# A quantized cross-attention product with a LoRA expert layer: the first five row tiles laid out anew

## What is computed

```
def fake_quant(x, scale, zp):
    q = clip(round(x / scale + zp), 0, 255)
    return (q - zp) * scale

xattn(x1, x2) = matmul(fake_quant(x1, ...), fake_quant(x2, ...))
ffn(x)  = x @ W_up.T  +  LoRA delta of the one expert that argmax(x @ gate_w.T + expert_bias) picks
x = x + tanh(g_xattn) * xattn(layernorm(x), ctx_4096)
x = x + tanh(g_ffn)   * ffn(layernorm(x))
```

## Time and profile before

| | |
|---|---|
| median of three runs | 960.24 us |
| the profiled execution: its own time | 959.95 us |
| the profiled execution: span of its instructions | 958.1 us |
| TensorE busy | 936.5 us (98% of the span) |
| VectorE busy | 472.3 us (49%) |
| ScalarE busy | 234.5 us (24%) |
| GpSimd busy | 17.1 us (2%) |

### The profile page before, as it was taken

How to read it: one execution, slowest core, us unless ns; L and a number is a source line. 1 busy time by engine, 2 the same in 40 slices (tenths; PEclk the granted TensorE clock), 3 DMA queues, 4 the chain that set the end, 5 groups by cost and what they waited for, 6 DMA issues and landing times.

```text
span 958.1 us, 12470 instructions
## 1 busy us (share of the span) xinstructions
PE 936.5 (98%) x5253; PEld 501.1 (52%) x5278; DVE 472.3 (49%) x1022; ACT 234.5 (24%) x196; POOL 17.1 (2%) x40
## 2 busy tenths in 40 slices
PE   3999999999999999999999999999999999999998
PEld 2444444444455555555555555555555555555554
DVE  7774757785884715343342615343342615343321
ACT  6975776777650100000000000000000000000000
POOL 0001100000000000000000000000000000000000
PEclk9999999999999999999999999999999999999999
DMA  8999987688652332222223233222223222121211
GB/s 350 422 405 406 377 318 271 227 302 290 221 152 88 111 110 44 88 44 89 44 89 88 66 111 45 88 44 88 45 88 88 61 72 44 45 45 44 44 44 44
DMA packets 77081, 135.26 MB, mean 141 GB/s; under 512 B 61936, under 2 KB 62080, under 8 KB 62720
## 3 DMA queue, kind: packets, MB, share of 16 engines
q1 hardware_dynamic: 71088, 92.74, 30.1%
q0 software_dynamic: 3488, 24.92, 6.7%
q10 hardware_dynamic: 2448, 16.78, 4.3%
HBM read 90.38 MB, written 29.37 MB: 125 GB/s over the span
## 4 chain that ended last, share of the span: by engine, by line
PE 96%; ACT 2%; DVE 1%; DMA 1%; issue 0%; SPq 0%; ACTq 0%
PE bank L1085 71%; PE bank L1003 22%; PE bank L1094 1%; PE bank L980 1%; ACT arena L414 1%; DMA rows<-in_x 1%; DVE bn L598 0%; ACT rows_T L402 0%; ACT halves L384 0%; PE bank L1077 0%; DVE arena L669 0%; SPq L282 0%; PE bank L1100 0%; DVE ln L602 0%; ACT ln L378 0%
## 5 line engine op out<-in xcount | busy, mean ns | idle before, releaser
L1085 PE MATMUL bank<-arena,rows_T 128*128 128x416 f16 (+1 forms) x3840 | 683.4, 339 | 0.0
L1085 PEld LDWEIGHTS bank<-arena,rows_T 128*128 128x128 f16 x3840 | 372.4, 97 | 304.3
L1003 PE MATMUL bank<-arena,rows_T 128*128 128x512 bf16 x999 | 222.8, 381 | 3.7 <-DVE arena L669 2.5
L1003 PEld LDWEIGHTS bank<-arena,rows_T 128*128 128x128 bf16 x1024 | 99.5, 98 | 120.6 <-issue 4.8
L783 DVE SCALAR_TENSOR_TENSOR rows<-bank,derived,rows 128x416 f32<-128x416 f32 (+2 forms) x80 | 49.8, 640 | 213.9 <-PE bank L1085 213.9
L453 ACT ACTIVATE z_stack_T<-bank 96x128 f16<-96x128 f16 x16 | 4.4, 273 | 560.1 <-PE bank L1100 560.1
L598 DVE BATCH_NORM_STATS2 bn<-rows 128x6 f32<-128x512 f32 x124 | 76.7, 678 | 5.9 <-DMA rows<-in_x 5.7
L723 DVE SCALAR_TENSOR_TENSOR route<-bank,derived,scal 128x4 f32<-128x4 f32 x16 | 3.5, 221 | 113.2 <-PE bank L1085 113.2
L659 DVE SCALAR_TENSOR_TENSOR rows<-bank,derived,rows 128x512 f32<-128x512 f32 x60 | 44.7, 748 | 25.0 <-PE bank L1003 24.6
L791 DVE SCALAR_TENSOR_TENSOR rows<-bank,z_back_scale,rows 128x512 f32<-128x512 f32 x64 | 45.1, 746 | 10.6 <-PE bank L1094 6.6
L699 DVE SCALAR_TENSOR_TENSOR halves<-normed,ln,halves 128x2048 f16<-128x2048 f32 x14 | 32.9, 2351 | 29.0 <-ACT halves L447 29.0
(11 more groups left out here) (106 smaller groups left out, 293.0 us busy)
## 6 DMA issues: line engine op xcount, KB each, us to landing
arena<-in_ctx SPq DMA_DIRECT2D x22, 1024.0 KB, 16.4
stage<-in_w SPq DMA_DIRECT2D x17, 1042.0 KB, 5.5
out<-rows ACTq DMA_DIRECT2D x15, 1024.0 KB, 3.9
h_scratch<-rows POOLq DMA_DIRECT2D x11, 1024.0 KB, 9.5
rows<-h_scratch SPq DMA_DIRECT2D x11, 1024.0 KB, 4.9
stage<-in_ctx SPq DMA_DIRECT2D x10, 1024.0 KB, 9.9
rows<-in_x POOLq DMA_DIRECT2D x10, 1024.0 KB, 9.2
normed<-in_w SPq DMA_DIRECT2D x7, 1042.0 KB, 6.5
```

The costliest lines, as they stand in the source:

```text
L1003: mm = mmul(bk, q1T[:, t % 4, kt, :], Q(b, n, kt), start=(kt == 0), stop=(kt == KT - 1 and not slow), skip_group_check=True)
L1085: mm = mmul(bank[c][:, 0:b - a], YT[:, s % 2, yh, kt, :], W(kt, wh, a, b), start=(first and kt == kts[0] and yh == 0 and wh == 0), stop=(k ...
```

## The change

It alters six things, all ahead of row tile 5:

- `BY_V` grows from three halves to six. VectorE copies halves (0,0), (1,0), (2,0), (2,1), (3,0) and (3,1). ScalarE keeps (0,1), (1,1) and both halves from tile 4 on.
- `order` is written out for the first 16 chunks, and TensorE's parts are single steps that mix up to four row tiles; whole chunks begin only at (4, 0).
- The eight zero products that stood between `transposes(0)` and `transposes(1)` stand ahead of `transposes(0)`.
- SP loads row tile 3 ahead of context tile 3, row tile 4 behind context tile 8 (it was behind 13) and row tile 5 behind 13 (it was behind 15).
- ScalarE and VectorE get new orders up to `ctx_round(19)` and `clip(5)`.
- `moments(2)` and `moments(5)` are split in two, so that other work stands between their halves.

```diff
@@ -37,7 +37,7 @@
     BY_PE = 2
     HALF = KT // 2
 
-    BY_V = [(1, 0), (2, 1), (3, 1)]
+    BY_V = [(0, 0), (1, 0), (2, 0), (2, 1), (3, 0), (3, 1)]
     SPARE = 5
     YS = 2.0 ** 9
     WS = 2.0 ** 14
@@ -53,9 +53,8 @@
     h_t = nc.dram_tensor("h_scratch", (TILES - KEEP, P, D), F32).ap()
 
 
-
-    order = [(t, n) for n in range(2) for t in range(LEAD)] + [(LEAD, 0), (LEAD, 1)] + [
-        (t, n) for a in (0, 2) for n in range(2, NCH) for t in (a, a + 1)] + [
+    order = [(1, 0), (0, 0), (2, 0), (2, 1), (0, 1), (3, 0), (1, 1), (2, 2),
+             (3, 1), (1, 2), (0, 2), (0, 3), (1, 3), (3, 2), (2, 3), (3, 3)] + [
         (t, n) for t in range(HEAD, TILES) for n in range(NCH)]
     place = {tn: g for g, tn in enumerate(order)}
     ROT = (0, 1, 2, 3, 4, 7)
@@ -286,18 +285,22 @@
             row(2)
             ctx_tile(1)
             ctx_tile(2)
+            row(3)
             ctx_tile(3)
-            row(3)
             ctx_tile(4)
             ctx_tile(5)
             ctx_tile(6)
             ctx_tile(7)
-            for c in range(8, 14):
-                ctx_tile(c)
+            ctx_tile(8)
             row(4)
+            ctx_tile(9)
+            ctx_tile(10)
+            ctx_tile(11)
+            ctx_tile(12)
+            ctx_tile(13)
+            row(5)
             ctx_tile(14)
             ctx_tile(15)
-            row(5)
             for c in range(16, CT):
                 ctx_tile(c)
             for i in range(KT + 8):
@@ -478,35 +481,38 @@
             quant(0)
             sqrt(1)
             ctx_round(0)
-            half(0, 0)
             quant(1)
             half(0, 1)
+            ctx_round(1)
             sqrt(2)
-            ctx_round(1)
+            ctx_round(2)
             quant(2)
             half(1, 1)
-            ctx_round(2)
-            half(2, 0)
             ctx_round(3)
             ctx_round(4)
             sqrt(3)
             ctx_round(5)
+            ctx_round(6)
             quant(3)
-            ctx_round(6)
             ctx_round(7)
             ctx_round(8)
-            half(3, 0)
-            for c in range(9, 15):
-                ctx_round(c)
+            ctx_round(9)
+            ctx_round(10)
+            ctx_round(11)
+            ctx_round(12)
+            ctx_round(13)
+            ctx_round(14)
             sqrt(4)
+            quant(4)
             ctx_round(15)
-            quant(4)
+            ctx_round(16)
             sqrt(5)
-            ctx_round(16)
+            ctx_round(17)
+            ctx_round(18)
             quant(5)
-            evac(4)
-            for c in range(17, 20):
-                ctx_round(c)
+            half(4, 0)
+            half(4, 1)
+            ctx_round(19)
 
             def period(p, a, b, c):
                 a()
@@ -800,63 +806,68 @@
 
             moments(0)
             quant_scale(0)
-            scalars()
             moments(1)
             clip(0)
             quant_scale(1)
-            moments(2)
+            scalars()
+            half(0, 0)
+            moments(2, 0, 2)
             clip(1)
-            quant_scale(2)
+            moments(2, 2, 4)
             ctx_clip(0)
             ctx_clip(1)
+            quant_scale(2)
+            half(1, 0)
+            ctx_clip(2)
             clip(2)
-            half(1, 0)
             moments(3, 0, 2)
-            ctx_clip(2)
-            half(2, 1)
+            half(2, 0)
             ctx_clip(3)
             moments(3, 2, 4)
+            ctx_clip(4)
             quant_scale(3)
-            ctx_clip(4)
+            half(2, 1)
+            epi(1, 0)
             ctx_clip(5)
+            clip(3)
             ctx_clip(6)
-            clip(3)
+            ctx_clip(7)
             epi(0, 0)
-            ctx_clip(7)
-            delta_parts()
-            epi(1, 0)
             ctx_clip(8)
+            half(3, 0)
             epi(2, 0)
+            epi(2, 1)
+            ctx_clip(9)
+            ctx_clip(10)
             half(3, 1)
             epi(0, 1)
-            ctx_clip(9)
-            epi(1, 1)
-            ctx_clip(10)
-            epi(2, 1)
-            epi(3, 0)
             ctx_clip(11)
             ctx_clip(12)
-            epi(3, 1)
+            epi(3, 0)
+            delta_parts()
             ctx_clip(13)
             moments(4)
+            moments(5, 0, 2)
+            quant_scale(4)
+            epi(1, 1)
+            epi(2, 2)
             ctx_clip(14)
+            epi(3, 1)
+            moments(5, 2, 4)
+            epi(1, 2)
+            ctx_clip(15)
             epi(0, 2)
-            quant_scale(4)
-            ctx_clip(15)
-            epi(1, 2)
-            moments(5)
+            ctx_clip(16)
             clip(4)
             epi(0, 3)
+            ctx_clip(17)
+            ctx_clip(18)
             quant_scale(5)
-            ctx_clip(16)
             epi(1, 3)
+            ctx_clip(19)
+            epi(3, 2)
+            epi(2, 3)
             clip(5)
-            epi(2, 2)
-            ctx_clip(17)
-            epi(3, 2)
-            ctx_clip(18)
-            epi(2, 3)
-            ctx_clip(19)
 
             def w_pow(n):
                 powers(n, n + 1)
@@ -1017,40 +1028,76 @@
                 pe.wait_ge(s_ve, 1)
                 zeros(6)
                 pe.wait_ge(s_idb, 1)
+                zeros(8)
                 transposes(0)
-                zeros(8)
                 transposes(1)
                 part(0, 0, 0, 1, slow)
                 part(0, 0, 1, 2, slow)
+                part(1, 0, 0, 1, slow)
+                part(1, 0, 1, 2, slow)
                 transposes(2)
-                part(1, 0, 0, 2, slow)
                 part(0, 0, 2, 3, slow)
                 part(1, 0, 2, 3, slow)
+                part(2, 0, 0, 1, slow)
+                part(1, 0, 3, 4, slow)
+                part(2, 1, 0, 1, slow)
+                part(2, 0, 1, 2, slow)
+                part(0, 1, 0, 1, slow)
+                part(2, 0, 2, 3, slow)
                 part(0, 0, 3, 4, slow)
-                part(2, 0, 0, 3, slow)
-                part(2, 1, 0, 1, slow)
-                part(1, 0, 3, 4, slow)
+                part(2, 0, 3, 4, slow)
                 part(2, 1, 1, 2, slow)
+                part(0, 1, 1, 2, slow)
                 part(1, 1, 0, 1, slow)
-                part(0, 1, 0, 1, slow)
-                part(0, 1, 1, 2, slow)
+                part(1, 1, 1, 2, slow)
+                part(1, 1, 2, 3, slow)
+                transposes(3)
                 part(2, 1, 2, 3, slow)
-                part(2, 0, 3, 4, slow)
-                part(1, 1, 1, 2, slow)
-                transposes(3)
-                part(1, 1, 2, 3, slow)
+                part(2, 1, 3, 4, slow)
+                part(2, 2, 0, 1, slow)
+                part(3, 1, 0, 1, slow)
+                part(1, 2, 0, 1, slow)
+                part(3, 0, 0, 1, slow)
                 part(0, 1, 2, 3, slow)
+                part(3, 1, 1, 2, slow)
+                part(3, 0, 1, 2, slow)
                 part(0, 1, 3, 4, slow)
+                part(3, 0, 2, 3, slow)
+                part(3, 0, 3, 4, slow)
+                part(2, 2, 1, 2, slow)
+                part(0, 2, 0, 1, slow)
+                part(0, 2, 1, 2, slow)
+                part(0, 2, 2, 3, slow)
+                part(0, 3, 0, 1, slow)
                 part(1, 1, 3, 4, slow)
-                part(2, 1, 3, 4, slow)
-                chunk(LEAD, 0, slow)
-                chunk(LEAD, 1, slow)
-                for a in (0, 2):
-                    for n in range(2, NCH):
-                        for t in (a, a + 1):
-                            chunk(t, n, slow)
-                    if a == 0:
-                        transposes(HEAD)
+                part(3, 1, 2, 3, slow)
+                part(2, 2, 2, 3, slow)
+                part(1, 2, 1, 2, slow)
+                part(2, 2, 3, 4, slow)
+                part(3, 1, 3, 4, slow)
+                part(0, 3, 1, 2, slow)
+                part(1, 2, 2, 3, slow)
+                part(1, 2, 3, 4, slow)
+                part(1, 3, 0, 1, slow)
+                part(1, 3, 1, 2, slow)
+                part(3, 2, 0, 1, slow)
+                part(3, 2, 1, 2, slow)
+                part(0, 2, 3, 4, slow)
+                part(0, 3, 2, 3, slow)
+                part(0, 3, 3, 4, slow)
+                part(2, 3, 0, 1, slow)
+                part(1, 3, 2, 3, slow)
+                part(2, 3, 1, 2, slow)
+                part(3, 3, 0, 1, slow)
+                part(3, 2, 2, 3, slow)
+                part(3, 3, 1, 2, slow)
+                transposes(4)
+                part(1, 3, 3, 4, slow)
+                part(2, 3, 2, 3, slow)
+                part(3, 2, 3, 4, slow)
+                part(3, 3, 2, 3, slow)
+                part(2, 3, 3, 4, slow)
+                part(3, 3, 3, 4, slow)
                 for t in range(HEAD, TILES):
                     for n in range(NCH):
                         chunk(t, n, slow)
```

## The result

The changed kernel takes **964.57 us** (median of six runs, 962.58 to 965.27) against 959.99 for the kernel before in the same runs: ratio 1.0045, 95% interval 1.0035 to 1.0055. That is 4.6 us slower, where 959.8 was forecast with 962.0 as the high end. The profiled execution took 964.51 us. Five executions of those behind this document, two of them of the kernel before, were disturbed and took 996 to 3555 us; no ratio counts them.

A forecast was written before the change was run, and what follows sets the result against it. TensorE was taken to bound the kernel. From the profiled 959.95, minus 1.4 for the start plus 0.95 for row tile 6 gave 959.5; with 0.29 for the median, 959.8 us, range 958.4 to 962.0.

The forecast's parts named there:

- What bounds the kernel: TensorE, busy 98% of the span; only its waits or slow running can be had, 23.6 us lost ahead of 34.89.
- The gate: Start of the kernel: context tile 4's clip sets TensorE's start; ready at 31.7 after the change, gain 1.4 us.
- Later steps: After context tile 4: no further TensorE wait up to the transposes of tile 5, which would begin at 85.35.
- Zeros at no cost: Start: moving the zero products ahead of the transposes of tile 0 costs nothing, or 0.6 if that cover is gone.
- rival C: Start: TensorE's products stay at 1.2 GHz up to tile 4, 4.8 us late, 963.6 us in all; chance 0.06.
- the cushion of 1.1 us: Start: TensorE waits about 1.1 us for context tile 4, room for slower products before it.
- Row tile 6: Later stores delay its load; it lands at 90.0, 1.75 later, and TensorE stalls 0.95 us for `clip(6)`.
- the load at about 79.2: GpSimd's queue: row tile 6's load is issued at about 79.2, after `store(1)` at 78.5.
- The sum of bytes: Transfers from 71.2, full at 413 GB/s: 7.5 MB in 18.8 us bring row tile 6 at 90.0.
- the upper bound: Latest landing of row tile 6: 93 at most, from 90.1 plus 2.5 us for `store(1)` still ahead.
- The fixed stretch behind the landing: VectorE: from row tile 6's landing to the end of `clip(6)` the code is unchanged, 11.0 us.
- Rival B: Row tile 6 becomes the bound, its load queued behind `store(1)`; landing at 93 means 4.0 us stall, 962.8; chance 0.09.

The follow-up runs named there:

- before_clip4: The kernel before, with only context tile 4 clipped ahead of `quant_scale(3)`: 960.01 us, ratio 1.0000.
- clip4_late: `row6_on_sp` with the clip of context tile 4 put back behind `quant_scale(3)`: 960.47 us, ratio 1.0006.
- row6_on_sp: The changed kernel, but SP holds context tiles from 20 on until tile 0's store has landed, then loads row tile 6 ahead of them: 958.69 us, ratio 0.9987.
- row6_warm: `row6_on_sp` with 12 more zero products between the transposes of tiles 0 and 1 and 4 behind them: 958.77 us, ratio 0.9994.
- zeros_old: `row6_on_sp` with the eight zero products back between the transposes of tiles 0 and 1: 958.80 us, ratio 0.9987.
- zeros_wait: The changed kernel with twenty zero products behind chunk (5, 0), to fill the wait for `clip(6)`: 962.79 us, ratio 1.0028.
- pool_first: The changed kernel with row tile 6 loaded ahead of the store of tile 1 on GpSimd's queue: 963.96 us, ratio 1.0037.
- late_stores: The kernel before, with only the stores of tiles 0 and 1 made to wait for 13 and 14 epilogues: 965.93 us, ratio 1.0056.
- sp_hold: The changed kernel, but SP asks for context tile 20 only when the store of tile 0 has landed: 965.05 us, ratio 1.0056.

## Why the prediction was wrong, point by point

**What bounds the kernel: right. The gate: right for the new list, not for the old one.** The loss of 23.6 us ahead of 34.89 holds. That the clip of context tile 4 set it does not: `before_clip4` takes this wait away and gains nothing. In the new list it does set the start, as `clip4_late` shows. The gain was put at 1.4 us; freed of row tile 6 it is 1.3 in time. In the trace of `row6_on_sp` it shows as 0.8, as context tile 4 is rounded from 29.36 in place of 28.8 and ready at 32.3 in place of 31.7.

**Later steps: right.** No wait stood between 33 and 86 in the changed kernel.

**Zeros at no cost, and rival C: right as to the time.** Low clock came, as rival C said, from about 19.8 to 26.6, but the cushion of 1.1 us at context tile 4 took it up: with low clock (`row6_on_sp`) or without it (`row6_warm`, `zeros_old`) the time is the same. In the changed kernel's profile itself, where it lasted 6.8 us, the four steps behind the transposes of tile 2 ran straight into context tile 4's. The rule of the Trainium skill ("TensorE: Matmul & The Clock Gate", Part 4: PE-mode transpose) that the gate does not engage for transposes was not tested by itself. The profiles show this much: all seven kernels without zeros between the transposes of tiles 0 and 1 had a stretch at 0.50 between 19 and 26 us. Of the five with zeros there, four stayed at 1.00 and one, the kernel before, did not (0.52 from 22 to 24). So zeros there help, and do not always prevent it.

**Row tile 6: the step that failed.** The steps up to the stores were good to 1.1 us: `store(0)` predicted at 71.8 came at 72.93, `store(1)` at 78.5 came at 79.60. The step that failed is "the load at about 79.2". It sets the load right behind `store(1)` and so puts the wait for `store(0)` to land at nothing, though the load may not go out before. The earlier trace rows held this wait: before, 77.38 - 67.63 = 9.75 us passed from the first store to the load. After, the store took 11.1 us to land and the load went out at 84.29, 5.1 us later than predicted. With the 9.7 of before, the prediction's own sum would have had the load at 81.5, its landing 10.9 later at 92.4, and a stall of about 3.3 us in place of 0.95.

The sum of bytes, on which the landing at 90.0 rested, failed too, by 3.4 us; the landing came 0.4 beyond the upper bound. The sum starts at 71.2, when context tile 19 was to land, and takes the transfers as full from there. But the new order of ScalarE puts `quant(4)` ahead of `ctx_round(15)`, which ends at 66.8; only then does SP ask for context tile 19 (61.6 before), and it landed at 73.7. From 71.2 to 77.5 the rate was 350 GB/s, not 413. Nor were 7.5 MB enough: 8.82 million bytes, as much as 8.4 loads of 1024 KB, passed from 71.2 to 93.4. (7.5 times 2.54 is also 19.0, not 18.8.) The fixed stretch behind the landing, 11.0 us to `clip(6)`, was right to 0.1. So the stall was 3.7 us, 0.4 of it at the half of tile 5, not 0.95.

**A term that was missing.** The stall was priced at its own length. The trace of the changed kernel has 1.7 us of low clock behind it, and `zeros_wait` takes it away. Rival B priced a landing at 93 with 962.8; with the clock it would have said 964.5, close to what was measured. Part of that is luck: its landing was 0.4 too early and its gain in the prologue 0.7 more than the profile shows. I gave it 0.09, for it needed "a third of the bandwidth lost to others".

**The mechanism in rival B was only half right.** I put it on `store(1)` and GpSimd's order. `pool_first` shows that the order is worth about 0.6 us. What decides is that `store(0)` itself goes out 5.3 us later and that row tile 6 may not be loaded before it has landed: its landing at VectorE moved by 5.1 us. The store then took 1.6 us longer to land than before (11.1 against 9.5) and the load 1.8 less (9.1 against 10.9). That context tiles are asked for sooner (tile 22 at 73.05 in place of 76.39, SP's timeline) is not needed for it: `late_stores` asks for them at the old times, and its store still took 11.7 us. `sp_hold` and `pool_first` show that neither cure works alone, and `row6_on_sp` that both together do.

## What to carry to other kernels

When an order is rearranged for the engine that bounds, follow each result that leaves: a block that finishes all its tiles late, and together, delays the stores that free the slots of the next loads. The whole delay of the store comes back as delay of the load, here 5.3 and 5.1 us. Follow the chain link by link, each with the time that the trace of before has for it: the link left out here, from the store's issue to the load's, stood there with 9.7 us. Compare the sum with the room that the first thing behind the rearranged part has, here 2.2 us at `clip(6)`. And put a price on a stall that includes the clock that may be low behind it: here 3.7 us of waiting cost 5.4 in the profile.

## What the runs showed of the hardware

- A store of 1 MB on GpSimd's queue took 4.4 us from issue to landing with SP's queue held back (`sp_hold`), and 11.1 us with three context tiles in flight or queued there (the changed kernel); it was 9.5 in the kernel before and 11.7 in `late_stores`. In the changed kernel all queues together moved 350 GB/s from 71.2 to 77.5 and 416 from 77.5 to 93.4:

```profile
77.50:93.40 15.90, 15.79 (x86) 7.66 (x86) 4.15 (x6) 5.55 (x4) 2.68 (x5) 1.00 1.01 416
```

- A wait of 3.2 us behind dense products was followed by 3.4 us at 1.2 GHz (granted clock 0.50) in the profiles of the changed kernel, `pool_first` and `late_stores`. In that of `sp_hold`, with a wait as long, and one of 2.3 us shortly ahead of it, it was not: the granted clock stayed at 1.00, and 14.71 us lie between the next two sets of transposes. Why not, no run here shows.

```profile
106.12 1.07 PE L993 MATMUL bank<-ident_bf,halves 128*128 128x128 bf16 x16 [3.19 <-DVE halves L660]
107.02 13.98 PE L1016 MATMUL bank<-arena,rows_T 128*128 128x512 bf16 x64
120.83 1.06 PE L993 MATMUL bank<-ident_bf,halves 128*128 128x128 bf16 x16
```
